# Two-layer attention and mixture kernel: the down product of every other layer-0 tile as three rounded products, behind a deeper pipeline

## The reference, cut to what matters

```
# layer 0, feed-forward (all 64 experts of width 64, and a shared one of width 128)
g = einsum('th,ehi->tei', x, Wg);  u = einsum('th,ehi->tei', x, Wu)
h = silu(g) * u * coef[:, :, None]
moe_out = einsum('tei,eih->th', h, Wd)
shared = silu(x @ SWg) * (x @ SWu) @ SWd
```

## Time and profile before

| | |
|---|---|
| median of 3 runs | 1770.86 us (1767.52 to 1775.95) |
| the profiled execution | 1774.19 us |
| its span, first to last instruction | 1772.6 us |
| PE busy | 1693.8 us, 96% of the span |
| DVE busy | 1324.0 us, 75% |
| ACT busy | 811.7 us, 46% |
| POOL busy | 610.3 us, 34% |
| mean granted TensorE clock | 0.985 of full speed |

### The profile page before, as it was taken

How to read it: one execution, slowest core, us unless ns; L and a number is a source line. 1 busy time by engine, 2 the same in 40 slices (tenths; PEclk the granted TensorE clock), 3 DMA queues, 4 the chain that set the end, 5 groups by cost and what they waited for, 6 DMA issues and landing times.

```text
span 1772.6 us, 24385 instructions
## 1 busy us (share of the span) xinstructions
PE 1693.8 (96%) x7020; PEld 1192.9 (67%) x7020; DVE 1324.0 (75%) x3818; ACT 811.7 (46%) x1457; POOL 610.3 (34%) x656
## 2 busy tenths in 40 slices
PE   6999999999999999999999999999999989888885
PEld 4677777777777777777777777777777666555553
DVE  4868788888888888888888888888888775543448
ACT  4535454545454545353535354545453535433321
POOL 4310232323232323232423232324231434555561
PEclk8999999999999999999999999999999999999998
DMA  8857555556565646464646464636363455666548
GB/s 221 187 129 215 139 151 134 156 129 161 122 167 120 170 115 175 109 181 106 184 99 173 95 177 93 176 93 176 87 173 93 114 158 181 199 194 218 169 140 305
DMA packets 172338, 273.88 MB, mean 155 GB/s; under 512 B 14312, under 2 KB 57320, under 8 KB 171952
## 3 DMA queue, kind: packets, MB, share of 16 engines
q1 hardware_dynamic: 163632, 254.63, 54.5%
q0 software_dynamic: 8576, 17.70, 3.1%
HBM read 202.15 MB, written 65.93 MB: 151 GB/s over the span
## 4 chain that ended last, share of the span: by engine, by line
PE 89%; DVE 3%; ACT 3%; another core or an unknown queue 2%; issue 2%; DMA 1%; POOL 1%; SPq 0%; ACTq 0%; DVEq 0%; POOLq 0%
PE ps_y L709 25%; PE ps_gate L662 8%; PE ps_gate L660 8%; PE ps_gate L661 8%; PE ps_up L660 7%; PE ps_up L662 7%; PE ps_up L661 7%; PE ps_y L735 3%; PE ps_side L675 3%; PE ps_side L852 1%; PE ps_side L758 1%; PE ps_side L835 1%; ACT silu_h L1317 1%; PE ps_side L794 1%
## 5 line engine op out<-in xcount | busy, mean ns | idle before, releaser
L918 DVE TENSOR_TENSOR silu_h<-ps_up,silu_h 128x512 f32<-128x512 f32 x618 | 425.4, 689 | 370.4 <-ACT silu_h L1317 263.2
L1317 ACT ACTIVATE silu_h<-ps_gate 128x512 f32<-128x512 f32 x618 | 368.0, 599 | 614.1 <-PE ps_gate L662 540.0
L709 PE MATMUL ps_y<-silu_h,w_dn 128*128 128x512 f32 x1056 | 540.5, 593 | 2.1 <-DVE silu_h L912 2.1
L912 DVE TENSOR_TENSOR silu_h<-coef_b,silu_h 128x512 f32<-128x512 f32 x528 | 388.4, 736 | 12.8 <-DMA coef_b<-coef_kept 8.5
L660 PE MATMUL ps_gate<-xnT,w_gu 128*128 128x512 f32 x528 | 340.8, 645 | 0.2 <-ACT silu_h L1317 0.2
L709 PEld LDWEIGHTS ps_y<-silu_h,w_dn 128*128 128x128 f32 x1056 | 199.5, 189 | 53.1 <-issue 7.7
L660 PE MATMUL ps_up<-xnT,w_gu 128*128 128x512 f32 x528 | 208.8, 395 | 6.6 <-DVE silu_h L918 6.6
L661 PE MATMUL ps_gate<-xnT,w_gu 128*128 128x512 f32 x528 | 209.0, 396 | 0.0
L662 PE MATMUL ps_gate<-xnT,w_gu 128*128 128x512 f32 x528 | 208.9, 396 | 0.0
L662 PE MATMUL ps_up<-xnT,w_gu 128*128 128x512 f32 x528 | 208.5, 395 | 0.0
L661 PE MATMUL ps_up<-xnT,w_gu 128*128 128x512 f32 x528 | 207.5, 393 | 0.0
(11 more groups left out here) (264 smaller groups left out, 2438.1 us busy)
## 6 DMA issues: line engine op xcount, KB each, us to landing
coef_b<-coef_kept SPq DMA_DIRECT2D x254, 512.0 KB
slots_x<-empty SPq DMA_DIRECT2D x15, 2080.0 KB, 12.6
w_block<-w_kept SPq DMA_DIRECT2D x45, 512.0 KB
xs<-slots_x SPq DMA_DIRECT2D x37, 260.0 KB
y_back<-y_kept SPq DMA_DIRECT2D x15, 512.0 KB, 7.1
w_down<-in_ffn_w SPq DMA_DIRECT2D x45, 128.0 KB
w_raw<-in_ffn_w SPq DMA_DIRECT2D x33, 128.0 KB, 4.8
xres<-in_x SPq DMA_DIRECT2D x16, 256.0 KB, 3.2
```

Source lines behind the costliest of these rows:

```text
L709: eng.matmul(ps_y[:, :], w_dn[:, j], silu_h[:, g % HBUFS], start=j == 0, stop=last).then_inc(pe_down)
L912: eng.tensor_tensor(silu_h[:, s], coef_b[:, q % COEF_RING, k], silu_h[:, s], ALU.mult).then_inc(dve_h)
L918: eng.tensor_tensor(silu_h[:, s], ps_up[g % 2][:, :], silu_h[:, s], ALU.mult).then_inc(dve_h1)
L1317: eng.activation(silu_h[:, s], ps_gate[g % 2][:, :], ACT.Silu).then_inc(act_silu)
```

## The change

- The down product of each tile with an odd number in its chunk (16 of 33, so 256 of 528) becomes three rounded products. ACT copies `silu_h` to a high part `h_hi` in fp32r (`h_round`, new), POOL subtracts to get the low part `h_lo` (`h_rest`, new). Each has one buffer; both wait until the down product of the odd tile before is done.
- The rounding of tile g - 3 stands at the head of step g on ACT (ahead of silu of tile g) and on POOL (ahead of the side work of step g, behind that of step g - 1).
- All down products of layer 0 stand four steps behind gate and up (before three); layer 1 keeps three. `silu_h` has 5 buffers (before 4).
- The down weights of odd tiles are split into high and low like gate and up, in the same "split", which is then 128x384 for odd tiles. Even tiles keep their fp32 weights in `w_dn`.
- "yT" and "y_add", the output of the chunk before, move by one tile: y_add from tile 4 to tile 5, where it stands ahead of x_lo0 and stats1.
- In the last chunk the eight sends of chunk 13 stand at tiles 10 to 17, one each; before at 10, 12, 14, 15, 16, 18, 20 and 21.
- Three thresholds of the last chunk, which tell when layer-1 rows and weights may be loaded over layer 0's weights, count down products instead of up products and are changed.
- The scratch for POOL's DMA descriptors is set to 2048 bytes a partition.

```
-LAG = 3
-TILES_UNDER_XS, TILES_UNDER_XST, TILES_UNDER_WEIGHTS = 9, 15, 27
-HBUFS = 4
+LAG0, LAG1 = 4, 3
+TILES_UNDER_XS, TILES_UNDER_XST, TILES_UNDER_WEIGHTS = 8, 12, 22
+HBUFS = 5
+HI_BUFS, LO_BUFS, SPLIT_LATE = 1, 1, 3
-FINISH0 = [(3, "yT"), (4, "y_add")]
+FINISH0 = [(4, "yT"), (5, "y_add")]
+ROUTE1_THEN = [(at, what) for at, what in ROUTE1 if not what.startswith("send")] + [(43 + n, f"send{n}") for n in range(TOP1 * ROWS)]
...
-        plan[g] += [(what, c - 2) for at, what in ROUTE1 if at == j + TILES0 and c > 1]
+        plan[g] += [(what, c - 2) for at, what in (ROUTE1 if c < SPARSE else ROUTE1_THEN) if at == j + TILES0 and c > 1]
...
     TensorE, last_products(g)
+                if odd(g):
+                    n, w = odd_before(g), weights0(j)[:, 2]
+                    hi, lo = h_hi[:, n % HI_BUFS], h_lo[:, n % LO_BUFS]
+                    eng.wait_ge(act_hhi, n + 1)
+                    eng.matmul(ps_y[:, :], w[:, 0], hi, start=False, stop=False)
+                    eng.matmul(ps_y[:, :], w[:, 1], hi, start=False, stop=False)
+                    eng.wait_ge(pool_hlo, n + 1)
+                    eng.matmul(ps_y[:, :], w[:, 0], lo, start=False, stop=False).then_inc(pe_down)
+                    return
...
     ScalarE
+            def h_round(g):
+                n = odd_before(g)
+                eng.wait_ge(dve_h, scaled_before(g) + 1)
+                if n >= HI_BUFS:
+                    eng.wait_ge(pe_down, odd_at(n - HI_BUFS) + 1)
+                eng.copy(h_hi[:, n % HI_BUFS], silu_h[:, g % HBUFS]).then_inc(act_hhi)
...
+                if odd(g - SPLIT_LATE):
+                    h_round(g - SPLIT_LATE)
                 if TILES_FIRST <= g < TILES + UNITS1:
                     silu(g)
...
     GpSimd
+            def h_rest(g):
+                n = odd_before(g)
+                eng.wait_ge(act_hhi, n + 1)
+                if n >= LO_BUFS:
+                    eng.wait_ge(pe_down, odd_at(n - LO_BUFS) + 1)
+                eng.tensor_tensor(h_lo[:, n % LO_BUFS], silu_h[:, g % HBUFS], f32(h_hi[:, n % HI_BUFS]), ALU.subtract).then_inc(pool_hlo)
...
             for g in range(STEPS):
+                if odd(g - SPLIT_LATE):
+                    h_rest(g - SPLIT_LATE)
                 for what, key in plan[g]:
                     step(what, key, g)
...
-    nc = bacc.Bacc("TRN2", target_bir_lowering=False, num_devices=1)
+    nc = bacc.Bacc("TRN2", target_bir_lowering=False, num_devices=1, dynamic_dma_scratch_size=2048)
```

74 lines of the change are left out of this document (47 added, 27 removed).

## The result

The changed kernel takes 1862.48 us (median of 4 runs, 1861.08 to 1864.84), the kernel before 1769.19 in the same measurement: a ratio of 1.0518, with a 95% interval from 1.0499 to 1.0537. It is 5% slower; the forecast was 1.5% slower, and the time lies above the range.

A forecast was written before the change was run, and what follows sets the result against it. PE was taken to bound the kernel (89% of the span). A chunk: -2.4 saved, +1.6 waiting at tile 7, +2.7 through DVE, so +1.9; in all +26 on 1774.2, scaled to 1797 us, range 1760 to 1834.

The forecast's parts named there:

- the place at tile 7: PE waits 1.6 us once a chunk for tile 3's low part, whose subtraction stands behind stats1 on POOL.
- The other places: Subtractions behind stats0, q_sin, q_min, the sends and the hear adds on POOL: no cost to PE counted.
- the stretch costed next: About tiles 14 to 26, where DVE is nearly full; costed by PE's waits up to tiles 23 and 30.
- near zero: At tile 31's down step, the margin of the subtraction behind POOL's hear adds; counted at nothing.
- around tiles 15 to 19 or 31: Sign of being wrong upward: PE also waiting there for POOL, behind the sends and the hear adds.
- The term for DVE: Up products waiting for DVE held up by subtractions, 0.45 us each: 1.3 by tile 23, 1.4 by 30, together 2.7.
- The upper bound of one meeting: A POOL subtraction meeting a DVE two-input operation delays DVE by between 0 and 0.69 us.
- The saving: Three rounded down products on PE save 0.15 us per odd tile, 2.4 us a chunk.
- Chunk 0: Larger weight splits on ACT and POOL against PE's saving: +1 us, from bounds of -2 and +6.
- Chunk 15: +1.9 us like the others, less 3.9 for the sends' wait; late next is DVE itself; sum -2.
- The items costed at nothing: Layer 1's later rows and earlier weights, fifth buffer and smaller descriptor scratch: 0 us.
- The one with full blocking: Rival: every subtraction blocks DVE in full, 0.69 us or more each; 1829 to 1850 us, chance 0.08.

The follow-up runs named there:

- eleventh experiment: Changed kernel with only ten tiles a chunk rounded (1, 3, 5, 7, 21 to 31 odd), POOL's side work still ahead of the subtraction: 1.0071 of the kernel before.
- second experiment: Changed kernel with POOL subtracting a constant table instead, and PE not waiting for the result: 1.0025 of the kernel before.
- sixth: Changed kernel with POOL's two small operations of stats1 issued behind the next subtraction instead of ahead of it: 1.0359 of the kernel before.
- ninth: Changed kernel, all sixteen tiles rounded, with five pieces of POOL's side work issued behind the next subtraction: 1.0378 of the kernel before.
- tenth experiment: Changed kernel with ten tiles rounded (none from 9 to 19) and five pieces of POOL's side work behind the subtraction: 0.985 of the kernel before.
- first experiment: Changed kernel without POOL's subtraction; the third product takes the high part again: 0.9734 of the kernel before.
- fifth: Kernel before plus everything of the change except the rounding and the three thresholds; all down products in fp32: 0.9985 of the kernel before.
- fourth experiment: Kernel before with only the eight sends of chunk 13 moved to tiles 10 to 17 of the last chunk: 0.9972 of the kernel before.
- third experiment: Changed kernel with POOL's subtraction replaced by a minimum with zero (one SBUF input), PE waiting as before: 1.0264 of the kernel before.

## Why the prediction was wrong

The sign, the two kinds of wait and the place at tile 7 are right; the size is a third of what came, and the other places of POOL's order were missed.

- **The step that failed: "The other places [...] I count them at nothing; those that are late fall in the stretch costed next, where DVE is late too."** Waits for POOL's order were forecast at 1.6 us a chunk and measured at 5.3 and 5.1. Tile 7 is right (1.84). The same rule, applied to the add of q_feat and to the hear adds, gives 1.0, 0.9 and 0.9 more, with 0.9 of their sum from two subtractions that a product of DVE held up, a cost that the prediction had on DVE's side alone. The hear adds were looked at ("near zero"), the add of q_feat isn't in the list at all; the last sentence of the prediction names waits "around tiles 15 to 19 or 31" as the sign of being wrong upward, and that is what came, but no chance and no price stood for it. And all places were read at the phase of the kernel before, while this side work waits for ACT, and ACT for DVE, which both run later behind PE once they have more to do. The add of q_feat started 1.20 us after the gate product of tile 14 before (682.70 in the earlier trace rows, the gate product at 681.50) and 2.27 after it now (728.35 and 726.08); the first hear add stood at 0.40 after the gate product of tile 28 (at 718.43) and stands at 2.97 (769.94, gate product at 766.97). In the kernel before:

```profile
718.83 1.29 POOL L1583 TENSOR_TENSOR msg<-msg 128x512 f32<-128x512 f32 x1 [17.44 <-ACT msg L1465]
```

  At the old phase the forecast would have been right: with the add of q_feat at 1.20 the low part would be ready at 1.20 + 1.28 + 1.28 = 3.8 us after that gate product, and PE wants it at 730.36 - 726.08 = 4.3. The eleventh experiment agrees: with ten tiles the engines are less late, and the waits at 29 and 31 shrink from 0.9 and 0.9 to 0 and 0.4, while the one behind the statistics stays to the hundredth. And the assumption that two waits in one stretch cost only one isn't true here: without any wait for POOL the up product waits in chunk 7 as long as in the change (second experiment), and with the wait at tile 7 gone all the others stay (sixth). Tiles 29 and 31 don't lie in DVE's full stretch, and tile 15 comes ahead of where PE waits for DVE.
- **The term for DVE: 2.7 a chunk** from 0.45 for each subtraction; measured 3.7 and 2.6, from 0.58. The sum came about right by luck, since its two halves were wrong in opposite ways: 1.3 was forecast up to tile 23, and with restarts 3.2 came (1.4 at tile 23 and 1.3 before it at tiles 20 and 22); 1.4 was forecast at tile 30, and 0.6 came at tiles 29 and 30. The upper bound of one meeting, 0.69, was wrong (0.96 to 1.07). Removing one place of POOL's order gave its wait back whole (sixth experiment), moving five pieces gave 1.6 us of the 5 expected, because the pieces met other subtractions and other work of DVE (ninth).
- **The saving: 0.15 for each rounded tile**, measured 0.197, which by itself would have made the kernel 0.8 us a chunk faster. The price was read from the starts around one down product; the distance between the first up products of two neighbouring tiles without side work holds all of it. The kernel before at tiles 27 and 28, and the tenth experiment, where the down product between them (tile 23's) is rounded:

```profile
717.27 0.40 PE L660 MATMUL ps_up<-xnT,w_gu 128*128 128x512 f32 x1
...
719.53 0.40 PE L660 MATMUL ps_up<-xnT,w_gu 128*128 128x512 f32 x1
```

```profile
707.69 0.40 PE L706 MATMUL ps_up<-xnT,w_all 128*128 128x512 f32 x1
...
709.76 0.39 PE L706 MATMUL ps_up<-xnT,w_all 128*128 128x512 f32 x1
```

  2.26 us became 2.07 here, and 2.25 became 2.05 between tiles 25 and 26 (the down product of tile 21).
- **Chunk 0: +1 forecast, +5.7 measured**, near the bound of +6. Without subtractions it takes 91.73 us (first experiment), so they cost 6.8 there, beside the splits of the weights on the same engine; POOL is busy for 57.86 of 98.56 us. By the views of PE's waits the low part waits 3.2 us for POOL there, the side product for DVE's `coef` 6.4 instead of 4.4, and the up product for DVE 6.7 instead of 5.1; the three add up to the 6.8. (The first experiment has the 5.1 and the 4.4, and the fifth, without any rounding, has 4.2 and 4.9: that part goes with the deeper pipeline, not with the rounding, and chunk 0 is no longer for it, 93.05 in both the fourth and the fifth.)
- **Chunk 15: -2 forecast, +3.5 measured.** The sends' wait is worth 3.9, to the tenth as forecast (fourth experiment), and DVE doesn't wait for landings there any more. Without subtractions the chunk takes 90.91, with them 101.03. "Late next is DVE itself" was right in kind, but had no number: the up product of tile 23 waits 4.91 for DVE, and a side product 2.49 for POOL's running sums of the routing, which stand behind subtractions.

```profile
1497.11 0.39 PE L866 MATMUL ps_side<-gsel,common 128*128 128x40 f32 x2 [2.49 <-POOL gbefore L1592]
1516.88 0.80 PE L692 MATMUL ps_up<-xnT,w_two 128*128 128x512 f32 x1 [4.91 <-DVE silu_h L959]
```

  Behind each of these two waits the granted clock is low, near the lower of its two levels (1.2 of 2.4 GHz), and PE's products start 0.43 us apart instead of 0.23. Busy time in the two stretches:

```profile
1497.50:1501.90 4.40, 4.40 (x12) 2.84 (x12) 4.40 (x13) 1.88 (x2) 1.91 (x2) 0.61 0.89 204
1516.88:1522.20 5.32, 5.32 (x14) 4.28 (x15) 4.16 (x13) 0.91 (x2) 1.40 (x3) 0.51 0.09 28
```

  The chunk's granted clock is 0.95, before 0.98. As an estimate, 5% of 101.03 us less 2% of 97.49 is 3 us, so most of the +3.5 can be the price of the clock behind waits; the prediction had no term for it.
- **The items costed at nothing:** the fifth buffer, the scratch and y_add at tile 5 cost nothing in the middle chunks, as said. The pipeline's wait of 1.0 us at the start of layer 1 (fifth experiment) wasn't foreseen, and the thresholds have no run of their own; in all layer 1 is 2.8 us shorter in the profile after.
- **The rivals.** The one with full blocking ended at 1850 and had 0.08; the time lies beyond it, by another mechanism. Of its two reasons, the phase of copy and coefficient product was right: meetings begin nearly together, which is the dearest case. What the Trainium skill says in "SBUF — State Buffer", section "Who interferes with whom", fits the row at 698.15, where the product waits for the whole subtraction, and speaks against this change as it did; the 0.58 for each subtraction lies between the 0.45 that was taken and the 0.69 or more of the rule taken whole. Its words take in POOL operations with one SBUF input too. The trace of the third experiment speaks against that for the products that begin inside such an operation (0.68 us at the median), and the measurement decides; the mean of all coefficient products is 798 ns, between 759 without the added operation and 896 with the subtraction, and what raised it wasn't taken apart.

In numbers, for chunk 7: forecast -2.4 + 1.6 + 2.7 = +1.9; measured -3.2 + 5.3 + 3.7 = +5.8 (6.5 by the chunk's own time, the rest in shorter gaps). Of the error of 4.6 us, 3.7 is waiting for POOL. In chunk 12 it is 5.1 and 2.6, and the chunk is 4.8 longer than before.

## What to carry to other kernels

A piece of work added to an in-order engine has to be placed against each piece of side work ahead of it, by that piece's row and by what it waits for, in every place where it recurs: a place "near zero" is worth its own subtraction, at the phase that the changed kernel will have, and three places of sixteen made most of the error. Side work that is moved behind one such piece stands ahead of the next and meets other work of the neighbour engine, and an engine that waits less reaches its next wait sooner (1.6 us a chunk gained where 5 had been counted). A product that saves little each time (0.197 us) should be used only where its helpers find room: ten tiles of 33, with the side work behind the subtractions, take 1.5% off, all sixteen add 5%.
